# One batch's worth of queue order: SyncE's transfers for the attention context regrouped, a reciprocal taken earlier on VectorE, a bias added a step earlier on GpSimd

## The reference

```python
mod = (_silu(c) @ wmod).reshape(8, 6, 1, -1)
h = _layernorm(x) * (1 + ca) + sa
# inside the attention block, for every batch b and head
Q = einsum('bsd,dhr,hre->bhse', LN(h), q_U, q_V) + q_b        # K and V alike
scores = where(causal, einsum('bhse,bhte->bhst', Q, K) * scale, -1e9)
ctx = einsum('bhst,bhtd->bhsd', softmax(scores), V)
h = h + ctx @ out_U @ out_V + out_b
h = h + gelu(LN(h) @ fc1_U @ fc1_V + fc1_b) @ fc2_U @ fc2_V + fc2_b
x = x + ga * h
# then a shared MLP and a mixture of 8 experts (top 2), gated and added to x
```

## Time and profile before

| | us |
|---|---|
| median of 3 runs | 699.83 (698.48 to 700.15) |
| the profiled execution | 706.22 |
| its span, first to last instruction | 704.5 |
| TensorE busy in it | 607.5 (86%) |
| VectorE busy | 450.2 (64%) |
| ScalarE busy | 408.1 (58%) |
| GpSimd busy | 301.2 (43%) |
| mean granted TensorE clock | 0.959 of full |

### The profile page before, as it was taken

One profiled execution on the slowest core, in us unless ns is written; L12 is line 12 of the kernel. 1 busy time (PEld: TensorE's weight loads), 2 busy tenths in 40 slices (PEclk: granted clock), 3 DMA queues, 4 the chain that ended last, 5 costly groups with the idle time before them and its releaser, 6 DMA issues.

```text
span 704.5 us, 16609 instructions
## 1 busy us (share of the span) xinstructions
PE 607.5 (86%) x5841; PEld 401.2 (57%) x5841; DVE 450.2 (64%) x1346; ACT 408.1 (58%) x718; POOL 301.2 (43%) x478
## 2 busy tenths in 40 slices
PE   3988888887888879778868977999897999999997
PEld 2643444443444434334324666766765999999993
DVE  5759888888899857767732878777673222222227
ACT  0432678687677758656658465676434555555550
POOL 4232334253443605232313438666671445545452
PEclk9999799999999989998989988999899999999999
DMA  9653142443343424340463411211236788878779
GB/s 196 196 168 87 57 131 101 141 140 111 120 154 121 148 84 153 118 133 28 146 178 112 131 44 55 81 51 49 66 94 189 216 226 222 240 224 226 230 217 316
DMA packets 85842, 100.40 MB, mean 143 GB/s; under 512 B 13808, under 2 KB 67736, under 8 KB 85664
## 3 DMA queue, kind: packets, MB, share of 16 engines
q1 hardware_dynamic: 76608, 86.53, 41.1%
q0 software_dynamic: 4544, 9.45, 3.7%
q10 hardware_dynamic: 4608, 3.35, 1.9%
HBM read 59.89 MB, written 37.31 MB: 138 GB/s over the span
## 4 chain that ended last, share of the span: by engine, by line
PE 46%; DMA 13%; DVE 12%; SPq 9%; issue 9%; ACT 6%; POOL 5%; POOLq 0%; ACTq 0%; DVEq 0%
PE ps_r L1543 7%; PE ps_s L1533 7%; PE ps_pv L1351 6%; DVE row_max L1735 6%; PE ps_pv L1429 4%; DMA arena<-slots_d 3%; PE ps_r L1289 3%; POOL slots_d L931 3%; PE ps_r L1294 3%; DMA k_d<-arena_early 2%; DMA arena<-y_d 2%; PE ps_s L1334 2%; SPq L612 2%; PE ps_s L1437 2%; SPq L609 2%
## 5 line engine op out<-in xcount | busy, mean ns | idle before, releaser
L1735 DVE TENSOR_REDUCE row_max<-ps_r 128x1 f32<-128x384 f32 (+3 forms) x384 | 211.4, 594 | 45.8 <-PE ps_r L1294 43.1
L1007 ACT ACTIVATE arena<-ps_s 128x1024 f32<-128x1024 f32 (+1 forms) x192 | 168.6, 882 | 86.8 <-PE ps_s L1334 85.1
L977 POOL DMA_INDIRECT y_d<-arena,target x78 | 74.9, 960 | 86.5 <-DVE arena L1942 74.3
L1351 PE MATMUL ps_pv<-arena 128*32 128x512 f32 (+3 forms) x1024 | 95.4, 471 | 0.0
L1289 PEld LDWEIGHTS ps_r<-ident_h,later_q 64*128 64x128 bf16 x768 | 24.7, 94 | 121.3 <-DVE row_max L1735 78.9
L1289 PE MATMUL ps_r<-ident_h,later_q 64*128 64x64 bf16 (+1 forms) x768 | 49.5, 206 | 42.7 <-DVE row_max L1735 42.3
L1938 DVE TENSOR_TENSOR arena<-ps_r,arena_early 128x256 f32<-128x256 f32 x39 | 16.6, 425 | 108.2 <-PE ps_r L1543 108.2
L931 POOL DMA_INDIRECT slots_d<-arena,slots x64 | 65.3, 1020 | 18.2 <-issue 18.2
L1294 PE MATMUL ps_r<-arena 48*128 48x384 bf16 (+3 forms) x512 | 70.8, 310 | 0.0
L1334 PE MATMUL ps_s<-arena 51*128 51x256 bf16 (+3 forms) x512 | 70.6, 310 | 0.0
L1543 PEld LDWEIGHTS ps_r<-arena 128*128 128x128 f32 x480 | 58.2, 192 | 1.5
(11 more groups left out here) (240 smaller groups left out, 1129.0 us busy)
## 6 DMA issues: line engine op xcount, KB each, us to landing
arena<-in_ew SPq DMA_DIRECT2D x30, 514.0 KB
ctx_d<-ctx_raw SPq DMA_DIRECT2D x32, 256.0 KB, 2.6
arena<-q_d SPq DMA_DIRECT2D x64, 96.0 KB, 2.7
arena<-k_d SPq DMA_DIRECT2D x64, 96.0 KB, 2.7
arena<-slots_d SPq DMA_DIRECT2D x39, 132.0 KB, 3.0
arena_early<-in_ew SPq DMA_DIRECT2D x9, 514.0 KB, 3.8
arena<-y_d SPq DMA_DIRECT2D x8, 512.0 KB, 6.8
q_d<-arena_early SPq DMA_DIRECT2D x8, 384.0 KB, 2.5
```

The source lines that it names most:

```text
L977: pool.indirect_dma_start(y_d[:], bass.IndirectOffsetOnAxis(ap=target[:, k, c:c + 1], axis=0), res[:, k, c, :], None).then_inc(put[k], 16)
L1007: act.activation(dst, src, ACT.Exp, scale=SCALE).then_inc(exp_done, 1)
L1351: mm = pe.matmul(ps_pv[32 * j:32 * j + 32, kt * P:S], v_sb[b % 2][:, kt, GROUPS * j + g, :], probs[:, p % 2, at:at + length], start=(kt == ...
L1735: dve.reduce_max(row_max[:, m % 2, js[0] % 2, j:j + len(js), i], src, AXIS.X).then_inc(max_taken, 1)
```

## The change

On SyncE, within a step, the order becomes: the context store of group `n - 2` first (it stood late), then in step `4b + 6` the sums' load alone, then in step `4b + 7` the load of `rec_rows` and the four of `ctx_t` (they stood a step earlier), then the store of the maxima, the store of the reciprocals, the K stack's stores, the stack loads, the load of the maxima, and the Q stack's stores. The stack loads come one group a step (steps `4b - 6` to `4b - 3`) where groups 0 and 1 shared a step. VectorE takes the reciprocal after unit 5, not after unit 10. GpSimd adds `out_bias` in step `4b + 2`, not `4b + 3`.

```diff
-NORM_EARLY = 3
+NORM_EARLY, BIAS_AT = 3, 2
@@ SyncE
-                    def load_ctx(b):
+                    def load_sums(b):
                         for k in range(2):
                             wait(sp, ctx_stored[k], 32 * (b + 1))
                         wait(sp, rec_ready, b)
+                        sums_d = ctx_d[b % 2].rearrange("(j r) g s -> r j g s", j=JH)[DH].rearrange("j g s -> j (g s)")
+                        sp.dma_start(sums[:], sums_d.rearrange("j (c s) -> j c s", s=HEADS * S // P)).then_inc(sum_loaded, 16)
+
+                    def store_rec(b):
+                        wait(sp, rec_ready, b + 1)
+                        wait(sp, rec_loaded, 16 * b)
+                        sp.dma_start(rec_d.rearrange("h (c s) -> (h c) s", s=HEADS * S // P), recs[:]).then_inc(rec_stored, 16)
+
+                    def load_rec_and_ctx(b):
+                        wait(sp, ctx_ready, b)
+                        wait(sp, rec_stored, 16 * (b + 1))
+                        sp.dma_start(rec_rows[:], rec_d.unsqueeze(1).to_broadcast([HEADS, DH, S])).then_inc(rec_loaded, 16)
                         cells = ctx_d[b % 2].rearrange("(j r) g s -> r j g s", j=JH)
-                        sp.dma_start(sums[:], cells[DH].rearrange("j g s -> j (g s)").rearrange("j (c s) -> j c s", s=HEADS * S // P)).then_inc(sum_loaded, 16)
-                        wait(sp, ctx_ready, b)
                         for j in range(JH):
                             sp.dma_start(ctx_t[DH * GROUPS * j:DH * GROUPS * (j + 1), :], cells[0:DH, j].rearrange("e g s -> g e s"))\
                                 .then_inc(ctx_loaded, 16)
-                    def move_rec(b):
...
                     def step(n):
-                        for g, later in ((0, 0), (1, 0), (2, 1), (3, 2)):
-                            b = batch_at(n, LOAD_AT + later)
-                            if b is not None:
-                                load_stack(b, g, "k" if b == 0 and g == 0 else "qk")
+                        if 0 <= n - 2 < NG:
+                            store_ctx(n - 2)
                         if batch_at(n, CTX_AT) is not None:
-                            load_ctx(batch_at(n, CTX_AT))
+                            load_sums(batch_at(n, CTX_AT))
+                        if batch_at(n, CTX_AT + 1) is not None:
+                            load_rec_and_ctx(batch_at(n, CTX_AT + 1))
                         if 0 <= n + LAG - 1 < NG:
                             store_max(n + LAG - 1)
-                        if batch_at(n, K_OUT_AT - 1) is not None:
-                            store_stack(batch_at(n, K_OUT_AT - 1), 0)
+                        if batch_at(n, CTX_AT) is not None:
+                            store_rec(batch_at(n, CTX_AT))
                         if batch_at(n, K_OUT_AT) is not None:
                             store_stack(batch_at(n, K_OUT_AT), 1)
...
-                        if 0 <= n - 2 < NG:
-                            store_ctx(n - 2)
+                        for g in range(GROUPS):
+                            b = batch_at(n, LOAD_AT + g)
+                            if b is not None:
+                                load_stack(b, g, "k" if b == 0 and g == 0 else "qk")
                         if 0 <= n + LAG - 1 < NG:
                             load_max(n + LAG - 1)
-                        if batch_at(n, CTX_AT) is not None:
-                            move_rec(batch_at(n, CTX_AT))
+                        if batch_at(n, K_OUT_AT - 1) is not None:
+                            store_stack(batch_at(n, K_OUT_AT - 1), 0)
@@ GpSimd
-                        b = batch_at(n, 3)
+                        b = batch_at(n, BIAS_AT)
@@ VectorE
-                            if u == 10 and batch_at(n, CTX_AT) is not None:
+                            if u == 5 and batch_at(n, CTX_AT) is not None:
```

## The result

The changed kernel took 711.38 us (median of 20 runs, 705.67 to 716.27), the kernel before 701.78 us beside it (20 runs, 698.48 to 711.79). The ratio is 1.014, 95% interval 1.012 to 1.017: slower by some 10 us, where 8 us less were forecast, and outside the range of 682 to 700. The profiled execution took 713.77 us, its span is 712.0 us against 704.5, and the mean granted clock of TensorE fell from 0.959 to 0.942.

What follows compares the result with a forecast made beforehand. VectorE and TensorE, handing each other a ring of three banks, were taken as the bound. Terms -3.1 - 4.8 - 0.5 + 0.2 = -8.2 us took 706.22 to 698.0, scaled to the runs' median 691.7 us; range 682 to 700.

Steps and rivals of the forecast that it cites:

- The sums, the wait itself: VectorE's wait for the sums at unit 5: 1.34 us in each of batches 0 to 4, 6.7 us in all.
- The sums, what the wait costs: Attention steps with VectorE's waits for the sums: 6.7 us of waits instead of 9.8, a term of -3.1 us.
- a halved wait that might leave the gate open: TensorE's clock in step 19: it might stay up, making the sum 2.6 us lower; not counted.
- The base: Whole kernel: waits read from one profiled execution of 706.22 us, the result scaled to the runs' median of 699.83 us.
- GpSimd: Steps behind the reciprocals: `ctx_n` starts at tick + 10.4, TensorE's waits in steps 16 and 24 go, -4.8 us.
- the room of 2 us behind `split_max`: GpSimd's `split_max` ends at tick + 14.5, some 2 us before TensorE turns the maxima, shortly before tick + 17.9.
- The moved bias: GpSimd in step 4b+2: the bias takes 1.26 us there, but nothing was counted for it.
- Context stores first: SyncE's context store of step 28 is issued some 0.9 us sooner behind the same transfers: -0.5 us.
- The tail: Batch 7: context transfers follow `rec_rows`, `ctx_n` comes some 2 us later, TensorE had not waited for it: +0.2 us.
- The slower one: Sums queue behind the K store: five batches wait 3.5 us each at unit 5, with clock loss: 712 us, chance 8%.

Runs made afterwards that it cites:

- before, repeated: The kernel before, unchanged, run and profiled a second time: 702.86 us, ratio 1.002.
- bias alone: The kernel before with only GpSimd's first bias moved from step 4b+3 to step 4b+2: 696.29 us, ratio 0.988.
- changed, last context early: The changed kernel with batch 7's four context transfers issued with its sums again, a step earlier: 707.66 us, ratio 1.007.
- before, early reciprocal: The kernel before, old queue order, with only the reciprocal moved from behind unit 10 to behind unit 5: 728.98 us, ratio 1.038.
- changed, with fillers: The changed kernel with six unused matmuls of 512 columns on TensorE in each step 4b+6, ahead of unit 8's scores: 697.91 us, ratio 0.990.
- their control without a wait: The kernel with the sums a step earlier, plus the same six unused matmuls in the steps 4b+6: 695.79 us, ratio 0.989.
- the kernel with the sums a step earlier: The changed kernel with the sums loaded in step 4b+5 behind the maxima's store, and batch 7's context transfers with its sums: 689.92 us, ratio 0.979.

## Why the prediction was wrong

**The sums, the wait itself: right.** 6.7 us were forecast for batches 0 to 4, 6.90 measured; batches 0 and 3 were to have 0.83 and 1.85 us and had 1.02 and 1.92. (The upper end of the term is written as +8.9; by the rival's own numbers, 17.7 - 9.8, it is 7.9.)

**The sums, what the wait costs: wrong, and this is the step that failed.** The term was -3.1 us. The five steps grew by 4.8 us against the profiled kernel before and by 12.0 against its repetition. The prediction charged a wait at unit 5 like one at unit 10, 1 us for each us, and let the clock stand as it was ("I do not count them as won"), at no more loss than before. The five steps against the same steps without a wait (44.9 us at the early place, 45.9 at the late, where 1.2 us are the slow stretch in step 7) give the prices:

| kernel | place | five waits, us | excess of five steps, us | us per us |
|---|---|---|---|---|
| before | unit 10 | 9.8 | 13.2 | 1.3 |
| before, repeated | unit 10 | 4.8 | 6.0 | 1.3 |
| bias alone | unit 10 | 10.2 | 10.8 | 1.1 |
| changed | unit 5 | 6.9 | 19.0 | 2.7 |
| changed, last context early | unit 5 | 7.8 | 19.1 | 2.5 |
| before, early reciprocal | unit 5 | 23.5 | 40.3 | 1.7 |
| changed, with fillers (4.3 us of them their own) | unit 5 | 4.7 | 5.1 | 1.1 |

The sums of five hide what a single wait does. Step by step, against the same step without a wait:

| kernel, step | place | wait, us | TensorE's pause, us | at the lower clock behind it, us | excess of the step, us |
|---|---|---|---|---|---|
| changed, 23 | unit 5 | 1.60 | 2.12 | 0 | 1.6 |
| last context early, 15 | unit 5 | 0.57 | 1.11 | 0 | 0.6 |
| before, repeated, 11 | unit 10 | 1.79 | 1.54 | 0 | 1.9 |
| bias alone, 15 | unit 10 | 1.64 | 1.39 | 0 | 1.5 |
| bias alone, 19 | unit 10 | 2.49 | 2.24 | 3 | 3.8 |
| last context early, 23 | unit 5 | 1.61 | 2.11 | 7 | 4.2 |
| changed, 11 | unit 5 | 0.88 | 1.42 | 10 | 4.8 |
| changed, 19 | unit 5 | 1.92 | 2.42 | 10 | 5.9 |

Where the clock stays, a wait costs about its own length at either place. What comes on top comes with the lower clock, which follows four of the five waits of the changed kernel, and none in batches 1 to 4 of the kernel before in its repetition (in batch 0 most kernels with the late reciprocal have some 3 us at the lower clock there, with a wait and without). The changed kernel's own counter-example is step 23: a longer pause than in step 11, and no fall (300.91 is the product behind the pause; the columns of the second row as in the earlier trace rows):

```profile
300.91 0.24 PE L1294 MATMUL ps_r<-ident_h,later_q 64*128 64x64 bf16 x4 [2.12 <-DVE row_max L1740]
```

```profile
301.00:312.00 11.00, 8.97 (x156) 4.65 (x157) 9.25 (x17) 8.33 (x11) 2.41 (x6) 1.00 0.35 114
```

So a pause of 2.12 us was followed by full clock here and one of 2.11 us by 7 us at the lower one in the experiment on the last context. What decides between them no run shows. The fillers, and their control without a wait, show that the excess beyond the waits goes when TensorE's pause is filled.

The place still matters, for how long TensorE stands. Behind unit 5 it has no product of probabilities and V to go on with, only the scores of units 8 and 9, which need the bank of unit 6: its pauses are some 0.5 us longer than VectorE's waits. Behind unit 10 it goes on with the scores and products that are ahead of it, and its pauses are 0.25 us shorter than the waits, as this row of the kernel before shows for the wait of 3.71 us:

```profile
257.95 0.39 PE L1289 MATMUL ps_r<-ident_h,later_q 64*128 64x128 bf16 x4 [3.46 <-DVE row_max L1735]
```

The prediction saw that difference and priced it at 0.5 us a batch. No run moved the reciprocal behind another early unit, so whether any place there would do better with the same wait is open.

The prediction cited "TensorE: Matmul & The Clock Gate" of the Trainium skill, in the part on the HAM clock gate, for a halved wait that might leave the gate open. The Trainium skill's rule there, that idleness closes the gate, agrees with the trace of step 11 (1.00 ahead of the pause of 1.42 us, 0.53 in the 11 us behind it). The inference that a shorter wait would be harmless does not: that pause, with one of 0.44 us before it, was enough.

**The base: partly of one execution.** The wait of 9.8 us was 4.8 in the repeated profile. Against that profile the account of the changed kernel is: five steps +12.0 us, steps 12, 16, 20, 24 and 25 -8.2 us, tail +4.1 us, all else +3.0 us (step 3, 1.6 us longer with the slow clock from 98 to 102, is half of it), which is the 10.9 us between the spans of 712.0 and 701.1. Against the first profile the same account is +4.8, -4.0, +4.1 and +2.6 us, together the 7.5 us between 712.0 and 704.5.

**GpSimd: the direction right, the start of `ctx_n` too early.** Forecast -4.8 us. Steps 24 and 25 shortened by 4.3 us against the profiled kernel before, and the steps 12, 16, 20, 24 and 25 together by 4.0 against it and by 8.2 against the repeated one; no wait of TensorE for `neg_part` is left. The bias alone gives about the same, 4.4 and 8.5 us. But `ctx_n` starts 11.2 to 12.1 us behind the tick in batches 0 to 4, not 10.4 (batch 1: 172.72 + 11.8 = 184.56), and the steps `4b + 7` of the changed kernel are long, which leaves it room. In the kernel with the sums a step earlier those steps take 8.5 to 9.1 us, `ctx_n` starts 11.5 to 13.6 us behind the tick, and TensorE waits for `neg_part` again in steps 20 and 24. So the room of 2 us behind `split_max` that the prediction reckoned is not there in undisturbed steps. The moved bias cost nothing that can be seen.

**Context stores first: nothing won.** The store of step 28 is issued sooner behind its tick, 358.95 - 354.86 = 4.09 us where it was 358.14 - 353.11 = 5.03, which is the 0.9 us of the forecast. But it takes longer to land than the second of the earlier trace rows, and step 29 takes 11.93 us against 11.38:

```profile
358.95 6.57 DMA ctx_d<-ctx_raw
```

**The tail: the mechanism half seen, the size wrong.** I said that `ctx_n` of batch 7 would come 2 us later and that TensorE does not wait for it. I looked at who waits for `ctx_n` and not at what is queued behind it on GpSimd: the mean squares of another batch, which the chain runs through. The piece after the load of `rec_rows` is the wait for the context transfers:

```profile
396.42 3.12 DMA rec_rows<-rec_d
399.54 4.04 issue
403.58 1.26 POOL ctx_n L883
404.84 1.67 POOL h_sb L898
...
407.48 1.03 POOL mlp_rstd L927
```

**The rivals.** The slower one named 712 us, and its nearness to the measured 711.4 is luck: its sums should have landed slowly behind the K store and waited 3.5 us each. In the changed kernel the sums of batch 1 were issued at 169.76 and were there at 172.28, 2.5 us, and its wait was 0.88. What it had right was a clock loss on the waits, 2.6 us each; measured are 12.1 us beyond the five waits (19.0 - 6.9), 2.4 each on average. It should have stood in the forecast itself. "DMA: Bandwidth & Descriptors" of the Trainium skill, in the section on queues, rings and completion order, had been cited for that rival with its rule that a ring is served in order; no run here shows the order within a ring, and the landing time of 2.5 us speaks against the rival's size once more.

## What to carry to other kernels

Where two engines hand each other a short ring, do not price a wait by its length alone: ask which bank the other engine wants next, and whether it still has other work. A short wait at a point where TensorE runs dry can cost several times its length, when the granted clock halves for some microseconds behind it, and it does not do so each time; give that loss a term and a chance of its own. So load the operand earlier before moving its use earlier. And when a transfer moves later, list what stands behind its consumer in that engine's program, not only who reads its result.

## What the chip showed that I had not expected

- A pause of TensorE of 1.42 us, behind one of 0.44 us, was followed by a granted clock of 0.50 for about 10 us in an otherwise dense stretch, and that step took 3.9 us longer than the same step with nearly the same wait and the pause filled. A pause of 2.12 us in the same kernel was followed by full clock.
- Added matmuls, 42 of 512 columns, took 2.4% off the time of a kernel, and cost 0.9 us a step (six of them) where there was no pause.
- Two profiles of one kernel differ in the sums' wait by a factor of two (9.8 and 4.8 us) and in the span by 3.4 us (704.5 and 701.1), which is nearly half of the 8.2 us that I forecast to win.
